# Spare matmuls in the layer normalisations of a twelve-sublayer decoder kernel

## The reference, cut to what matters

```
def _layernorm(x, axis=-1, eps=1e-05):
    m = jnp.mean(x, axis=axis, keepdims=True)
    v = jnp.var(x, axis=axis, keepdims=True)
    return (x - m) / jnp.sqrt(v + eps)
```

## Time and profile before

| | |
|---|---|
| runs | 1935.27, 1936.41, 1938.59 us; median 1936.41 |
| profiled execution | 1938.32 us, of it 1936.4 from the first to the last instruction |
| mean granted clock of TensorE | 0.87 of full speed |
| busy: TensorE matmul, VectorE, ScalarE, GpSimd | 82%, 68%, 54%, 31% |
| MATMUL records | 8,925 |

### The profile page before, as it was taken

One profiled execution on the slowest core, in us unless ns is written; L12 is line 12 of the kernel. 1 busy time (PEld: TensorE's weight loads), 2 busy tenths in 40 slices (PEclk: granted clock), 3 DMA queues, 4 the chain that ended last, 5 costly groups with the idle time before them and its releaser, 6 DMA issues. The chain is left out here.

```text
span 1936.4 us, 26938 instructions
## 1 busy us (share of the span) xinstructions
PE 1590.5 (82%) x8925; PEld 965.5 (50%) x8933; DVE 1308.1 (68%) x2693; ACT 1039.6 (54%) x2055; POOL 603.3 (31%) x543
## 2 busy tenths in 40 slices
PE   6967899999999787999968778764999877449834
PEld 3743466666677453665643456452222434228613
DVE  3766877676676344888467469347999766854667
ACT  2113556555554225889457568225999732535524
POOL 0405443231300002889244030013990000425700
PEclk9989999999999998999989889897555588779958
DMA  5100000000000101111035240007999800020000
GB/s 214 29 1 27 1 1 1 1 1 1 1 1 1 46 17 34 45 44 55 1 72 99 50 87 2 25 35 194 183 182 183 150 22 6 0 87 1 2 0 22
DMA packets 213689, 93.20 MB, mean 48 GB/s; under 512 B 205968, under 2 KB 206992, under 8 KB 211888
## 3 DMA queue, kind: packets, MB, share of 16 engines
q1 hardware_dynamic: 213408, 91.10, 20.6%
q10 hardware_dynamic: 144, 0.39, 0.1%
HBM read 39.49 MB, written 1.11 MB: 21 GB/s over the span
## 5 line engine op out<-in xcount | busy, mean ns | idle before, releaser
L1052 POOL TENSOR_TENSOR ss_u<-dx,b_rows 128x512 f32<-128x512 f32 x128 | 158.9, 1273 | 242.6 <-POOLq L184 226.3
L2028 ACT ACTIVATE qc_p<-qc_s,qc_bias,sq 128x1024 int16<-128x1024 f32 x128 | 154.0, 1203 | 17.3 <-DVE qc_bias L1994 6.6
L1134 DVE TENSOR_TENSOR_SCAN ss_h<-ss_decay,ss_u 128x512 f32<-128x512 f32 x128 | 146.5, 1204 | 24.4 <-PE ss_ht L1092 16.9
L771 ACT ACTIVATE gq_p<-gq_s,gq_bias,gq_rq 128x512 f32<-128x512 f32 x128 | 98.4, 773 | 118.8 <-DVE gq_bias L841 118.7
L704 POOL TENSOR_TENSOR gq_xw<-gq_x,weights 128x512 f32<-128x512 f32 x48 | 67.9, 1415 | 292.4 <-ACT gq_x L731 291.7
L1992 DVE TENSOR_REDUCE qc_mx<-qc_s 128x1 f32<-128x1024 f32 x128 | 155.4, 1214 | 5.1 <-PE qc_s L1927 5.1
L1927 PE MATMUL qc_s<-kT,qT 64*128 64x512 bf16 x256 | 130.8, 617 | 14.2 <-ACT qc_p L2028 6.9
L1106 PE MATMUL ss_acc<-ss_hc,consts 128*128 128x512 f32 x256 | 131.0, 595 | 0.0
L639 PE MATMUL gq_s<-gq_KT,gq_QT 128*128 128x512 f32 x256 | 121.3, 596 | 3.6 <-ACT gq_p L771 3.6
L661 PE MATMUL gq_o<-gq_pT,gq_V 128*128 128x256 f32 x512 | 121.2, 379 | 1.4 <-DVE gq_pT L875 1.4
L838 DVE TENSOR_REDUCE gq_mx<-gq_s 128x1 f32<-128x512 f32 x128 | 88.3, 691 | 43.5 <-PE gq_s L639 43.0
(11 more groups left out here) (612 smaller groups left out, 3831.4 us busy)
## 6 DMA issues: line engine op xcount, KB each, us to landing
b_rows<-b_rows SPq DMA_DIRECT2D x16, 512.0 KB, 3.7
weights<-in_weights SPq DMA_DIRECT2D x1, 6152.0 KB, 17.3
weights<-in_weights SPq DMA_DIRECT2D x1, 5248.0 KB, 16.7
weights<-in_weights SPq DMA_DIRECT2D x1, 3072.0 KB, 9.7
weights<-in_weights SPq DMA_DIRECT2D x1, 2156.0 KB, 7.5
qc_pT<-qc_p SPq DMA_TRANSPOSE x128, 3.3
weights<-in_weights SPq DMA_DIRECT2D x1, 1410.0 KB, 9.1
weights<-in_weights SPq DMA_DIRECT2D x1, 1282.0 KB, 5.8
```

The source lines that it names most:

```text
L771: nc.scalar.activation(pr[c % 2][:, t, :], sc[t][:, :], ACT.Exp, bias=bias[:, c, t:t + 1], scale=rq[b % 2][:, t, u:u + 1], accum_out=sm[:, ...
L1052: nc.gpsimd.tensor_tensor(u_in[i % 3][:, :], dx[:, m, hf * HT:hf * HT + HT], rows.rows[c % 2][:, n % rows.NEACH, :], ALU.mult).then_inc(in ...
L1134: nc.vector.tensor_tensor_scan(h[group % 2][:, m, :], decay[i % 2][:].rearrange("p b t -> p (b t)"), u_in[i % 3][:, :], 0.0, ALU.mult, ALU ...
L2028: nc.scalar.activation(pi[i % R][:, :], sc[i % 3][:, :], ACT.Exp, bias=bias[:, i:i + 1], scale=sq[:, t, h:h + 1], accum_out=sm[:, i:i + 1] ...
```

## The change

`spin` issues n matmuls whose stationary operand is the identity and whose moving operand is the first columns of the context CT, as many as the bank is wide. All are f32, each overwrites the bank, and nothing reads it.

```diff
+def spin(g, bank, n):
+    for _ in range(n):
+        g.nc.tensor.matmul(bank[:, :], g.ident, g.CT[:, 0, 0:bank.shape[1]], start=True, stop=True)
+
 def layer_norm(g, weights=None, out=None):
...
         ps = [pb(f"ln_ps{i}", [P, 4, P]) for i in range(4)]
+        spare = pb("ln_spare", [P, 512])
...
                 def _(pe):
+                    spin(g, spare, 5)
                     for i in range(4):
                         c, half = i % 2, i // 2
                         pe.wait_ge(x_ready, 4 * half + 4)
                         for j in range(4):
                             last = nc.tensor.transpose(ps[i][:, j, :], X[:, 4 * half + j, c * P:c * P + P], g.ident)
                         last.then_inc(turned, 1)
+                    spin(g, spare, 2)
...
-                fin.turn(0)
-                fin.turn(1)
+                fin.turn(0, pv)
+                fin.turn(1, pv)
...
-                fin.turn(0)
-                fin.turn(1)
+                fin.turn(0, sc[2])
+                fin.turn(1, sc[2])
...
-    def turn(self, half):
+    def turn(self, half, spare=None):
         nc, g = self.g.nc, self.g
+        if spare is not None:
+            spin(g, spare, 3)
         nc.tensor.wait_ge(self.x, 4 * half + 4)
         for c in range(2):
             if half == 1:
...
             last.then_inc(self.turned, 1)
+        if spare is not None and half == 1:
+            spin(g, spare, 2)
```

## The result

The changed kernel takes 1949.13 us (median of 6 runs, 1945.91 to 1953.28), the kernel before 1936.72 beside it (6 runs). The ratio is 1.0065 with a 95% interval of 1.0052 to 1.0078: slower by 12.4 us, about 5 more than forecast and inside the range. The profiled execution has a span of 1949.0 us against 1936.4, so the two profiles differ by the same amount as the medians, and can be compared stage by stage.

A forecast was written before the change was run, and what follows sets the result against it. The prediction saw TensorE busiest (82%), but each normalisation bounded by VectorE's chain, then TensorE's half-clock transposes. Terms 5.4 + 0.8 + 0.15 + 1.2 gave +7.55 us, a median of 1944.0 us, range 1937 to 1951.

The forecast's parts named there:

- its own case: Whole kernel: spares cost +7.55 us, median 1944.0, own range 1940 to 1949; chance 0.67.
- the margin kept for falls of the clock: Whole kernel: range stretched up to 1951 towards low clock under spares, each fall adding about 2.0 us.
- For four of them I take the clock as staying up: Normalisations after L0_attn, L0_ffn, L1_attn, L2_attn: clock stays 1.00 under the spares; each that falls adds about 2.0 us.
- a low clock under these spares: Sign that the prediction is wrong: half clock under the spares after L0_attn, L0_ffn, L1_attn and L2_attn.
- nobody waits for a spare: All engines but TensorE: no new instruction on VectorE, ScalarE, GpSimd, SyncE or DMA queues, and no waiting for spares.
- The 1.9 that the prediction had for the low clock: L1_xattn: with the clock low, spares end at 1099.1, past the wait's end at 1098.41, and the stage grows +1.9 us.
- a rise 4 us after the first spare: Normalisation after L0_xattn: starting at 0.50, clock rises after 4 us of TensorE work; +2.35 us, between +0.35 and +3.3.
- partly so: Rival: L2_attn begins at 1.00 and half of L1_ffn's low stretch is saved, -2.9 us each: 1938; chance 0.14.
- the next stages owe their clock to the trailing spares: Rival: trailing spares, not transposes, raise the clock, saving about 2 us in each of five places: 1933.9; chance 0.01.
- the first rival: Clock carries over into the next sublayers, shortening low stretches in L1_ffn, L2_attn and L3_ffn: -10.7 us, 1925.7; chance 0.08.
- One record per spare: Rival: a spare leaves one record, not two, so five fit the slot in 2.15 us: -6.8 us, 1929.6; chance 0.02.
- the clock falls in all four places: Rival: clock falls before the spares in the other normalisations too, 4 x 2.0 and 2 in L1_ffn: 1954; chance 0.08.

The follow-up runs named there:

- e1: The changed kernel with spares only in the five normalisations with a stage of their own, none inside the attention stages: 1949.64 us, 1.0058 to the kernel before.
- e3: The changed kernel without the two trailing spares behind the transposes, at all eight places: 1940.92 us, 1.0011 to the kernel before.
- e5: The changed kernel with four trailing spares instead of two in the five normalisations of their own: 1955.02 us, 1.0085 to the kernel before.
- e6: The changed kernel with all 59 spares 32 columns wide instead of 512 or 256: 1939.28 us, 1.0002 to the kernel before.
- e2: The changed kernel with only the 24 spares inside L1_xattn, L1_ffn and L3_xattn: 1936.54 us, 0.9990 to the kernel before.
- e7: The changed kernel with three leading spares in five own-stage normalisations and each turn of L1_xattn and L1_ffn, none trailing or in L3_xattn: 1937.45 us, 0.9995.
- c1: The kernel before, unedited, run again as a kernel of its own for its profile: 1938.09 us, 0.9995 to the kernel before.

## Why the prediction was right, and where it was too small

**Direction and mechanism held.** Each f32 spare leaves two records 0.43 us apart at the full clock (ten in 4.53), the first transposes are late, the transposes and copies get the full clock and win less than that, the trailing spares are last in the stage, and in this profile the next sublayers get nothing. e1, e3, e5 and e6 each bear on one of these: where the loss sits, that the trailing spares end the stage (twice), and that it is the length of the spares that costs. The number is less well met than the range says: 1949.13 lies at the upper end, just past the 1940 to 1949 that the prediction gave its own case; the margin kept for falls of the clock took it in.

**Term by term**, forecast and measured in the profile: after L0_attn +1.15 and 1.22; after L0_ffn +0.8 and 0.85; L3_xattn +1.2 and about 1.3; after L0_xattn +2.35 and 3.04; after L1_attn +0.55 and 2.28; after L2_attn +0.55 and 2.47; L1_xattn +0.8 and 2.32; L1_ffn +0.15 and -0.55. Forecast 7.55, measured 12.9 in these eight; the rest of the span sums to almost nothing.

**The step that failed** is the sentence "For four of them I take the clock as staying up, since TensorE is silent only for about 2.2 us". Two of the four fell, and cost 1.7 and 1.9 more; the price I had put beside it, 2.0 each, was right, the choice was not. The evidence lay in the earlier trace rows: in L0_ffn's case the clock was low 2.6 us after TensorE stopped, hardly more than those 2.2. In the four profiles with five leading spares (the change, e1, e3, e5) the clock was low under the spares in 9 of 16 such places, never after L0_attn. That is more than two of the four on average, where the sum had none. The prediction had named a low clock under these spares as a sign that it is wrong, and for this step it is.

**The second miss** is "nobody waits for a spare". For L1_xattn I priced the spares on TensorE's own list and left out ScalarE's, where the root of half 1 stands behind the copies of half 0. That is 2.3 instead of 0.8, when the clock is low. The 1.9 that the prediction had for the low clock came from another path, spares that outlast the wait of the second turn; in the trace they end at 1108.77, before it. In L0_xattn's normalisation the forecast took a rise 4 us after the first spare; it came at 654.0, 5.3 us after.

**The rivals.** In the changed kernel's profile the clock did not carry over: L1_ffn's first matmul, at 1114.31, met 1.00, but from 1114.8 to 1125.0 it was 0.50, and L2_attn began at 0.50 (1238.8 to 1244.4), with silences of 3.0 and 3.5 us before them. It can, however: in e5, after the same 3.5 us, L2_attn began at 1.00 (1243.4 to 1249.0), and its projections were 2.90 us shorter, just what the rival "partly so" gave for them; of the five profiles with full-width spares in L1_ffn (the change, e2, e3, e5, e7) it is the only one. That the next stages owe their clock to the trailing spares is refuted by e3: nothing stands behind the transposes there, and the next stage starts at the full clock. The Trainium skill says of transposes (page "TensorE: Matmul & The Clock Gate", section "Part 4: PE-mode transpose") that the full clock does not engage in transpose mode. The trace of the kernel before disagrees: from 149.25 the 16 transposes were all that TensorE did before the clock rose, at 153.05. In e3 the clock was up before the transposes, so it says less on that. (What the first rival calls "the same page" is this page.) "One record per spare" fell with the count of 9,043. That the clock falls in all four places happened in no profile; in that of the change it fell in two, in that of e1 in three.

## What to carry to other kernels

A spare matmul is a gain only if it ends before the wait that it fills, at the clock that it may meet. Look up the shortest wait, divide by the price at the half clock too, and follow the queue of every engine that reads what comes late. Nothing spare belongs behind the last useful matmul of a block whose end waits for every engine. And a gain of a quarter of a per cent (4.65 of 1936 us) that is bought through the clock needs more than one profile, since the same program moves by up to 3.6 us in single stages from one execution to the next (L3_ffn, the kernel before in its first profile and in c1).

## What the runs showed of the hardware

- The clock can fall when TensorE is already at work again: after L2_attn the spares began at 1305.04, 2.17 us after TensorE had stopped, and the clock was at 0.50 from 1306.0 to 1309.2.
- Pauses of the same length end differently. TensorE stopped for 2.16 us ahead of the spares after L0_attn and for 2.24 after L1_attn; the clock stayed in the first case and was low in the second.
- Transposes can bring the clock up: before, it rose from 0.50 to 1.00 at 153.05 with nothing on TensorE since 149.25 but 16 of them. Nothing is needed behind them: in e3 the next stage starts at the full clock.
- Ten f32 records of 32 columns take 1.27 us at the full clock and 2.31 at the half (e6, after L1_attn and after L0_attn), from start to start 0.11 and 0.21 us. Those of 512 columns are 0.43 and 0.85 apart. A sixteenth of the columns takes about a quarter of the time at either clock.
